# A graph attention layer on one core: loops written out, and indirect DMAs that take their index columns from the tables

## The reference

```python
h = relu(layernorm(x))
x_src, x_dst = h @ W_src.T, h @ W_dst.T
alpha = leaky(sum(x_src[src] * a_s) + sum(x_dst[dst] * a_d))     # per head
a = exp(alpha - segment_max(alpha, dst)); a = a / segment_sum(a, dst) * edge_weight
out = segment_sum(x_src[src] * a, dst) + bias
h1 = layernorm(out + h)
out = x + layernorm(h1 + gelu(h1 @ W1.T + b1) @ W2.T + b2)      # hidden width 1024
```

## Time and profile before

| | |
|---|---|
| time, median of 3 runs | 3507.52 us (3506.67 to 3513.02) |
| the profiled execution: its time, its span | 3504.29 us, 3502.4 us |
| busy: PE (20244 matmuls), DVE, POOL, ACT | 3087.5, 2394.6, 1882.2, 1793.7 us |
| chain that ended last: DVE, PE, issue, ACT, POOL, DMA | 25%, 21%, 19%, 17%, 13%, 2% |
| granted TensorE clock, mean | 0.973 of full speed |

### The profile page before, as it was taken

How to read it: one execution, slowest core, us unless ns; L and a number is a source line. 1 busy time by engine, 2 the same in 40 slices (tenths; PEclk the granted TensorE clock), 3 DMA queues, 4 the chain that set the end, 5 groups by cost and what they waited for, 6 DMA issues and landing times.

```text
span 3502.4 us, 61805 instructions
## 1 busy us (share of the span) xinstructions
PE 3087.5 (88%) x20244; PEld 2769.8 (79%) x20244; DVE 2394.6 (68%) x6449; ACT 1793.7 (51%) x3444; POOL 1882.2 (54%) x1833
## 2 busy tenths in 40 slices
PE   3777456499999999999999999999999999999998
PEld 3666445388888888888888888888888888888887
DVE  4555479657666666677776776667677777667766
ACT  3555412255555555555555555555555555555554
POOL 4777556355555555555555555555555555555552
PEclk9989879799999999999999999999999999999999
DMA  4333347512211211112222211221211222122210
GB/s 120 108 105 108 74 114 180 139 44 61 55 55 55 55 55 55 55 55 55 57 58 63 61 55 55 55 55 55 55 55 55 55 56 58 56 62 55 61 43 25
DMA packets 114328, 236.30 MB, mean 67 GB/s; under 512 B 20262, under 2 KB 69318, under 8 KB 114063
## 3 DMA queue, kind: packets, MB, share of 16 engines
q1 hardware_dynamic: 82446, 154.93, 14.4%
q0 software_dynamic: 31616, 77.97, 10.0%
HBM read 153.97 MB, written 78.91 MB: 66 GB/s over the span
## 4 chain that ended last, share of the span: by engine, by line
DVE 25%; PE 21%; issue 19%; ACT 17%; POOL 13%; DMA 2%; SPq 1%; POOLq 0%; DVEq 0%; ACTq 0%; another core or an unknown queue 0%
PE ps_f L1147 9%; DVE act_lo L1042 6%; ACT ps_f L694 6%; ACT arena L714 4%; ACT h L700 4%; DVE arena L968 4%; DVE arena L982 3%; DVE xt_lo L995 3%; POOL xb L550 3%; ACT act_hi L693 3%; DVE arena L1034 3%; POOL arena L605 3%; PE ps_t L1194 3%; POOL arena L594 3%; PE ps_a L1162 2%
## 5 line engine op out<-in xcount | busy, mean ns | idle before, releaser
L1042 DVE TENSOR_TENSOR act_lo<-ps_f,act_hi 128x512 fp32r<-128x512 f32 x784 | 540.8, 690 | 777.6 <-ACT ps_f L694 770.7
L693 ACT ACTIVATE act_hi<-ps_f,hidden_bias 128x512 fp32r<-128x512 f32 x784 | 536.4, 684 | 915.0 <-PE ps_f L1147 776.1
L1162 PE MATMUL ps_a<-ffn_hi,act_hi 128*128 128x256 f32 x3136 | 884.8, 282 | 20.3 <-DVE arena L1008 15.5
L1163 PE MATMUL ps_a<-ffn_lo,act_hi 128*128 128x256 f32 x3136 | 875.6, 279 | 0.0
L1164 PE MATMUL ps_a<-ffn_hi,act_lo 128*128 128x256 f32 x3136 | 873.9, 279 | 0.0
L1162 PEld LDWEIGHTS ps_a<-ffn_hi,act_hi 128*128 128x128 f32 x3136 | 590.0, 188 | 71.1 <-issue 40.6
L1147 PE MATMUL ps_f<-zt_hi,ffn_hi 128*128 128x512 f32 x1568 | 628.4, 401 | 11.8 <-DVE act_lo L1042 11.8
L1147 PE MATMUL ps_f<-zt_lo,ffn_hi 128*128 128x512 f32 x1568 | 620.6, 396 | 0.0
L1147 PE MATMUL ps_f<-zt_hi,ffn_lo 128*128 128x512 f32 x1568 | 620.2, 396 | 0.0
L1163 PEld LDWEIGHTS ps_a<-ffn_lo,act_hi 128*128 128x128 f32 x3136 | 589.0, 188 | 31.7
L1164 PEld LDWEIGHTS ps_a<-ffn_hi,act_lo 128*128 128x128 f32 x3136 | 589.5, 188 | 0.0
(11 more groups left out here) (160 smaller groups left out, 5884.1 us busy)
## 6 DMA issues: line engine op xcount, KB each, us to landing
xb<-in_x SPq DMA_DIRECT2D x98, 512.0 KB, 5.7
out<-arena SPq DMA_DIRECT2D x98, 512.0 KB, 4.0
msgs<-arena SPq DMA_DIRECT2D x49, 256.0 KB
arena<-msgs SPq DMA_DIRECT2D x49, 256.0 KB
sums<-arena SPq DMA_DIRECT2D x49, 256.0 KB
arena<-line SPq DMA_DIRECT2D x49, 128.0 KB
arena<-sums,idx POOLq DMA_INDIRECT x392
xb<-in_x,idx POOLq DMA_INDIRECT x196
```

What stands on the lines that cost most here:

```text
L693: act.activation(act_hi[:, m % AB, :], ps_f[:, m % 2, :], ACT.Gelu, bias=hidden_bias[:, m:m + 1]).then_inc(act_hi_ready, 1)
L1042: dve.tensor_tensor(act_lo[:, m % AB, :], ps_f[:, m % 2, :], act_hi[:, m % AB, :].bitcast(F32), ALU.subtract).then_inc(act_lo_ready, 1)
L1162: pe.matmul(to, act_hi[:, m % AB, cols], ffn2[0][:, m, :], start=(m == 0 and t % 2 == 0), stop=False, skip_group_check=True)
L1163: pe.matmul(to, act_hi[:, m % AB, cols], ffn2[1][:, m, :], start=False, stop=False, skip_group_check=True)
```

## The change

The pair loop, the sum loop and the scatters are written out on all engines, so that every position is a constant. The index column of an indirect DMA is then a constant slice of the table (`edge_ends`, `records`, `node_rows`), and the copies into `idx` and `slot`, their semaphores and the waits on them are gone, in the node stage too.

```diff
-        PAIR_LOOP = (XB, max(XB, XB * ((NPAIR - 4) // XB)), XB)
-        SUM_LOOP = (SB, max(SB, SB * ((NPAIR - 3) // SB)), SB)
+        PAIR_LOOP = (NPAIR, NPAIR, XB)
+        SUM_LOOP = (NPAIR, NPAIR, SB)
...
                 b = j.off % XB
                 wait_count(pool, gathered[b], 64 * j.before(XB))
                 pool.sem_inc(pool_gate, 1)
-                pool.tensor_copy(idx[:, b, :], edge_ends[:, bass.ds(2 * j.n, 2), :].rearrange("p c o -> p (c o)")).then_inc(idx_copied, 1)
-                pool.wait_ge(idx_copied, j.n + 1)
                 for t in range(TG):
                     wait_count(pool, h_ready, TG * (j.n - XB) + t + 1)
                     pool.sem_inc(pool_gate, 1)
-                    at = 2 * (t % 2) + 1 - t // 2
+                    at = edge_ends[:, 2 * j.n + t % 2, 1 - t // 2:2 - t // 2]
                     pool.indirect_dma_start(xb[:, b, t, :], None, x,
-                                            bass.IndirectOffsetOnAxis(ap=idx[:, b, at:at + 1], axis=0)).then_inc(gathered[b], 16)
+                                            bass.IndirectOffsetOnAxis(ap=at, axis=0)).then_inc(gathered[b], 16)
...
-                pool.tensor_copy(slot[:, b, :], records[:, bass.ds(c.n, 1), :].rearrange("p c o -> p (c o)")).then_inc(slot_ready, 1)
-                pool.wait_ge(slot_ready, c.n + 1)
-                pool.sem_inc(pool_gate, 1)
-                pool.indirect_dma_start(row_of[b], bass.IndirectOffsetOnAxis(ap=slot[:, b, 0:1], axis=0),
-                                        slot[:, b, 1:2], None).then_inc(rows_stored[b], 16)
+                pool.indirect_dma_start(row_of[b], bass.IndirectOffsetOnAxis(ap=records[:, c.n, 0:1], axis=0),
+                                        records[:, c.n, 1:2], None).then_inc(rows_stored[b], 16)
...
-            steps(pool, place, 0, NCH, RB, max(RB, RB * (NCH // RB)), RB)
+            steps(pool, place, 0, NCH, NCH, NCH, RB)
...
-                pool.tensor_copy(idx[:, g.par, :], node_rows[:, bass.ds(TG * g.n, TG)]).then_inc(idx_copied, 1)
-                pool.wait_ge(idx_copied, NPAIR + g.n + 1)
-                pool.sem_inc(pool_gate, 1)
-                for t in range(TG):
+                for t in range(TG):
+                    at = node_rows[:, TG * g.n + t:TG * g.n + t + 1]
                     pool.indirect_dma_start(rec[:, g.par, t, :], None, sums,
-                                            bass.IndirectOffsetOnAxis(ap=idx[:, g.par, t:t + 1], axis=0)).then_inc(rec_in[g.par], 16)
```

More of the change, by code:

```diff
@@ L163, in build @@
         node_rows = sb("node_rows", [P, NT], I32)
-        idx = sb("idx", [P, XB, TG], I32)
-        slot = sb("slot", [P, RB, 2], I32)
         xt = [sb(f"xt_{n}", [P, KC, GR], F32R) for n in ("hi", "lo")]
@@ L275, in build @@
          flag_sum, flag_pe, flag_done, all_in, num_ready, rank_step, ranked, moved_copied, sorted_out, sorted_in, in_order,
-         cols_ready, rows_cleared, empty_set, empty_stored, idx_copied, stat_step, x_stats, x_prepared, x_pow, x_scaled,
+         cols_ready, rows_cleared, empty_set, empty_stored, stat_step, x_stats, x_prepared, x_pow, x_scaled,
          h_ready, xt_turned, xt_hi, xt_lo, xs_done, xs_out, base_ready, msg_made, alpha_step, cand_ready, cand_turned, cand_copied,
@@ L279, in build @@
          vals_ready, eq_ready, agg_done, agg_out, den_step, rec_step, rec_made, target_ready, target_step, node_rows_set,
-         slot_ready, sp_gate, pool_gate, act_gate, dve_gate, node_rows_in,
+         sp_gate, pool_gate, act_gate, dve_gate, node_rows_in,
          n_stats, n_prepared, n_pow, n_scaled, nh_ready, nt_turned, nt_hi, nt_lo, lifted,
@@ L286, in build @@
          flag_sum flag_pe flag_done all_in num_ready rank_step ranked moved_copied sorted_out sorted_in in_order
-         cols_ready rows_cleared empty_set empty_stored idx_copied stat_step x_stats x_prepared x_pow x_scaled
+         cols_ready rows_cleared empty_set empty_stored stat_step x_stats x_prepared x_pow x_scaled
          h_ready xt_turned xt_hi xt_lo xs_done xs_out base_ready msg_made alpha_step cand_ready cand_turned cand_copied
@@ L290, in build @@
          vals_ready eq_ready agg_done agg_out den_step rec_step rec_made target_ready target_step node_rows_set
-         slot_ready sp_gate pool_gate act_gate dve_gate node_rows_in
+         sp_gate pool_gate act_gate dve_gate node_rows_in
          n_stats n_prepared n_pow n_scaled nh_ready nt_turned nt_hi nt_lo lifted
@@ L583, in gather_records @@
                 pool.sem_inc(pool_gate, 1)
-                pool.tensor_copy(idx[:, g.par, :], node_rows[:, bass.ds(TG * g.n, TG)]).then_inc(idx_copied, 1)
-                pool.wait_ge(idx_copied, NPAIR + g.n + 1)
-                pool.sem_inc(pool_gate, 1)
                 for t in range(TG):
+                    at = node_rows[:, TG * g.n + t:TG * g.n + t + 1]
                     pool.indirect_dma_start(rec[:, g.par, t, :], None, sums,
-                                            bass.IndirectOffsetOnAxis(ap=idx[:, g.par, t:t + 1], axis=0)).then_inc(rec_in[g.par], 16)
+                                            bass.IndirectOffsetOnAxis(ap=at, axis=0)).then_inc(rec_in[g.par], 16)
             def first_rstd(n):
```

## The result

The changed kernel takes 3675.97 us (median of 4 runs, 3668.17 to 3678.33) against 3507.32 (median of 4 runs, 3506.67 to 3513.02): 1.0473 times as long, with a 95% interval of 1.0453 to 1.0493. The profiled execution took 3668.17 us, 163.9 more than that of before.

A forecast was written before the change was run, and what follows sets the result against it. It took POOL to bound the pair stage and, in the node stage, the path PE awaits at `turn_z`; 3504.3 - 28 - 4 + 181 = 3653, with the median 3.2 above: 3656 us, range 3465 to 3700.

The forecast's parts named there:

- The gap g: Delay from a small POOL operation to an indirect DMA without a copy between: 0.65 us pair stage, 0.30 node stage.
- Pair stage, -28: POOL's round shrinks from 7.12 to 6.73 us; 40 looped and 9 written-out pairs gain 28 us.
- Sum stage, -4: Writing out the sum loop saves about 0.44 us at each of 10 turns, 4 us.
- Scatters and longer code, 0: Shorter scatters gain nothing since POOL idles 28.21 us behind them; longer code costs 0 to 7 us, taken as 0.
- Node stage, +181: Earlier POOL TENSOR_TENSORs hold two of DVE's four `finish` operations; the path to PE is 1.93 us later in 94 groups.
- The border of 1.4 us: Node stage: two `finish` operations are held if POOL's first big TENSOR_TENSOR starts under 1.4 us behind the first.
- rival 1: The gap stays 0.85 us everywhere, so only the fourth `finish` operation is held: 3468 us, chance 0.13.
- PE's idle time before `turn_z`: Node stage: PE's wait before the `turn_z` transposes grows from 0.86 us to over 2 a group.
- rival 2: Node stage: DVE's `finish` operations (L1034) aren't held, gaining 68 us there: 3407 us, chance 0.08.
- Rival 3: Node stage: a wait elsewhere on the path to PE absorbs the delay, leaving the front's gain: 3475 us, chance 0.05.

The follow-up runs named there:

- only the node copy out: The kernel before, loops and other copies kept, with the index copy taken out of the node stage alone: 3693.15 us, 1.0509 of before.
- two small copies: The changed kernel with two small unused 128x4 copies on POOL in front of `first_residual`: 3442.84 us, 0.9822 of before.
- three in most groups: The changed kernel with three small unused 128x4 copies on POOL in front of `first_residual`: 3452.39 us, 0.9836 of before.
- the node copy back: The changed kernel with the index copy in front of the node stage's gathers put back: 3498.24 us, 0.9963 of before.
- the residual out of the way: The changed kernel with POOL's `first_residual` moved right behind `input_residual`, ahead of `second_rstd` and the gathers: 3411.5 us, 0.9716 of before.
- six copies: The changed kernel with six small unused 128x4 copies on POOL in front of `first_residual`: 3479.52 us, 0.9913 of before.
- both orders: POOL's `first_residual` ahead of `second_rstd` and gathers, DVE's `first_stats` ahead of `act_rest` 0: 3358.5 us in the changed kernel, 3364.28 in the kernel before.
- loops only: The kernel before with pair loop, sum loop and scatters written out and every index copy kept: 3500.23 us, 0.9985 of before.

## Why the prediction was right, point by point

The time, 3676, lies 20 us above the predicted 3656 and inside the range of 3465 to 3700. The 20 us are three terms: the front gave 21 us and not 32 (11), the node stage cost 185 and not 181 (4), and the median lies 7.8 us above the profiled execution and not 3.2 (5). The ends that the prediction worked out were 3593 and 3718; why its range stops at 3700 it does not say.

- **The gap g.** In the pair stage 0.65 was predicted and measured. In the node stage I had taken 0.30 and it is 0.18. The picture behind it (0.85 us of preparation from the moment that the instruction ahead is handed over, hidden by a long one) fits both: behind `shift` 0.85 - 0.20, behind 1.01 and 2.39 us almost nothing. The rule that the prediction weighs, that of the Trainium skill, "Perfetto Trace Analysis", section "DMA Instruction — SWDGE (GPSIMD)", by which the sequencer decodes on once an instruction waits in the queue, would by its reading have made it 0 in the pair stage; the trace, with 0.65, disagrees.
- **Pair stage, -28.** The last norm came 24.2 earlier: rounds of 6.77 instead of 6.73 (2 us), and the loops' part 7.9 instead of 8.6. 2.3 of it are lost at once. DVE's last messages wait 4.65 us for the store of earlier ones, where it was ACT before. The scatters have just begun, which I hold for the reason but did not test. Another 2.0 of the gain are lost until the first sum is written; that I did not trace.
- **Sum stage, -4.** It was -1.6. **Scatters and longer code, 0.** Both right: POOL now idles for 83.22 us behind the scatters, until the sums are stored, where it was 28.21, and the node stage is the same 30.47 us a group with the loops written out or kept.
- **Node stage, +181.** It was 185. The mechanism was right in each link but one: two of the four `finish` operations held, L1033 behind them without a wait, L596 at 9.22 (predicted 9.12). The held ones are the second and the third, not the last two, because L609 comes at 0.79 and not at 0.97. That the length comes out nearly the same (6.43, predicted 6.33) is in part luck: the earlier residual takes 0.18 away, and the fourth operation, which now runs free behind the held third, adds some 0.4. The border of 1.4 us, on which the choice between the forecast and rival 1 rested, fits what is seen behind gathers: with the residual at 1.3, in one group here and three of the run with only the node copy out, two are held, and at 1.7 to 1.8 one. It is no border behind copies, where at 1.27 only one is held.
- **PE's idle time before `turn_z`.** Wrong. I had it grow from 0.86 us to over 2; it stayed 0.83 (72.6 / 88). The delay appears earlier on PE, at L1138 and L1153, 0.89 and 0.85 us a group, where PE waits for the late L1033 and for L999 of the same chain. The sum is 2.56 us a group against 1.12 before (80.9, 15.5 and 8.7 us at the three places, by the waits of before), which is 1.44 more. The whole node stage grew by 1.97 us a group (185 / 94), and the other 0.5 is PE's own work: it is busy for 2739.53 us instead of 2690.57, 0.52 a group, with the slower matmuls of the last section. They do not make the group longer: with only the node copy out the matmuls are the faster ones, and it is 30.47 us all the same, with more waiting on PE (250 us at the three places from 700 to 3400 us, against 225).
- **Rivals.** Rival 1 (one operation held, 3468) and rival 2 (none, 3407) did not happen here, but the experiments made both: 3443 to 3498 with one held (two small copies, three in most groups, or the node copy back), 3412 with the residual out of the way. With six copies none of the four is held either, but L983 is, and it was 3480. Rival 3 is refuted, since nothing absorbed the delay.

What was wrong in the argument beside that is why `finish` is held: two operands in SBUF are not needed. It made no difference to the number.

## What to carry to other kernels

Before an instruction is taken out of an engine's queue, look at what moves up behind it, and what the other engines do at that moment: here 1.3 us less on POOL put two 2.4 us operations onto the same moment as DVE's on SBUF, and cost 2 us in each of 94 groups. In this kernel the large GpSimd operations on SBUF belong where VectorE works from PSUM, waits, or computes statistics; moving them there was worth 264 us in the changed kernel and 78 in the one before, and moving one more piece of work off the path another 53 and 70. Time that hides such a collision (a copy, a wait) looks like waste in a profile, so a gap should be closed and the order set free in the same step.

## What the runs showed that I had not expected

**Matmuls of two speeds.** PE's L1163 and its counterparts (`ffn_lo`, `act_hi`, 128x256), by lines, between 1000 and 3000 us, in four kernels: before, changed, with two small copies, with six.

```profile
L1163 PE MATMUL ps_a<-ffn_lo,act_hi 128*128 128x256 f32 x2248 | 627.6, 279 | 0.0
```

```profile
L1154 PE MATMUL ps_a<-ffn_lo,act_hi 128*128 128x256 f32 x2101 | 593.1, 282 | 0.0
```

```profile
L1157 PE MATMUL ps_a<-ffn_lo,act_hi 128*128 128x256 f32 x2282 | 645.2, 283 | 0.0
```

```profile
L1157 PE MATMUL ps_a<-ffn_lo,act_hi 128*128 128x256 f32 x2253 | 629.5, 279 | 0.0
```

It is 279 ns or 282 to 283, and so in all twelve experiments: 279 in the kernel before and in the six variants that keep the small tiles `idx` and `slot` (96 bytes a partition) or have a spare tile of 48 or 96 bytes in their place; 282 or 283 in the changed kernel and in the six variants with 0 or 32 bytes there. These tiles lie right ahead of the matmuls' operands `xt`, `zt`, `act_hi` and `act_lo`, so what differs with them is the operands' address. The length of the code does not go with it (loops only: 279). Where PE is the bound it counts: with both orders a group takes 27.18 us in the changed kernel and 26.98 in the kernel before, some 19 us in all. That is where most of the front's gain went. Where PE waits for others, as in the changed kernel, it costs nothing that can be seen (30.47 us a group either way). The granted clock is 1.00 from 1000 to 3000 us in both kernels with both orders, so it is not the clock. That the address is the cause is a correlation over fourteen kernels; the changed kernel with both orders and 96 bytes of padding, which by it would take some 3340 us, was not run.

**A gap that depends on what stands ahead.** In the changed kernel an indirect DMA starts 0.65 us behind an operation of 0.20 us, 0.18 behind one of 1.01, and 0.30 behind another gather. Taking 1.04 us of copy and gap away therefore gave 0.35 in the pair stage.

**Two kinds of groups from one order.** In the kernel before, with only the loops written out and with the node copy back the residual starts at 2.1 or at 1.8 us, with 23, 80 and 85 of 94 groups of the early kind, and nothing in between. No run tells what chooses; it moves the whole time by 7 us or so, as much as the loops.
